# Attention and mixture-of-experts block: another order of work, and the gates sent to all partitions straight from one partition

## The chip, the cores and the metric

The kernel runs on one core of one Trainium2 chip. TensorE (PE) multiplies, VectorE (DVE), ScalarE (ACT) and GpSimd (POOL) do the rest, and SyncE (SP) issues nearly all DMAs; ACT issues a few. The metric is the time on the device in microseconds. Before the change it is 143.56 us (median of 3 runs, 143.04 to 144.24).

## The reference, cut to what matters

The input x is 4 sequences of 512 tokens of 128 values. Two residual steps follow each other:

```python
x = x + layernorm(attention(layernorm(x)))       # one head, width 128, softmax over 512 keys
x = x + layernorm(ffn(layernorm(x)))

# ffn, per token
cont   = sigmoid(h @ W_enc + b_enc) @ W_s2c + b_s2c          # 128 -> 256 -> 64
probs  = softmax(cont @ Wr + br)                             # 8 experts
gate   = the 2 largest of probs, scaled to sum 1, else 0     # [tokens, 8]
y_e    = relu(cont @ W1[e] + b1[e]) @ W2[e] + b2[e]          # 64 -> 128 -> 64, every expert
out    = sigmoid(sum_e gate[:, e] * y_e @ W_c2s + b_c2s) @ W_dec + b_dec
out    = layernorm(out) * ln_g + ln_b
```

All eight experts are computed for all tokens, and the gate scales each one's hidden layer.

## The kernel before

Each engine has its own list of instructions, written out by hand; semaphores tie them together, and no engine looks past an instruction that waits. A sequence b (0 to 3) is worked on whole: its 512 tokens are 4 tiles of 128. Attention of sequence b+2 is laced with the expert stage of sequence b, so that PE always has work; sequences 2 and 3 are left over at the end and make up the last stretch, from about 94 us on.

The change touches mainly the way of the gates. On DVE `router_top` and `router_gates` compute `gate`, 128 tokens by 8 experts for each tile. PE turns it (`turn_gates`), and ACT copies it to `gateT` (`gate_out`, L518): 8 partitions, one for each expert, with 512 floats (2 KB) in each. DVE multiplies the hidden layer of expert e, 128 partitions by 512 tokens, by the gates of that expert, so it needs that row of 512 on all 128 partitions: `gate_all[:, b % 2, e]`, two sequences deep. SP brings it there:

```python
sp.wait_ge(a_gT, b + 1)
sp.dma_start(gates_dram[b].ap(), gateT[0:E, b % 2]).then_inc(d_gate_out, 16)
sp.wait_ge(d_gate_out, 16 * (b + 1))
for e in range(E):
    sp.dma_start(gate_all[:, b % 2, e:e + 1],
                 gates_dram[b].ap()[e:e + 1].partition_broadcast(P))...
```

That is one write of 16 KB to memory (L357), a wait for it, and eight transfers of 256 KB (L362), each of which reads one row of 2 KB 128 times from memory and writes it to 128 partitions. A sequence moves 2 MB so.

`gate_hidden(b, e)` on DVE (L1158) waits for row e and for PE's hidden layer (L841, `hidden_pair`), writes `gated`, and frees both the hidden banks and, at e = 7, the buffer of rows. PE's `expert_out(b, e)` (L862) waits for `gated`. Behind `expert_out(b, 7)` PE has the scores of sequence b+3 (L729), `to_cont`, `to_spikes`, `route` for sequence b+1 and later its `turn_gates`. Behind `gate_hidden(b, 7)` DVE has the next `router_top` and `router_gates`. So the gates of sequence b+1 come after all of sequence b's expert stage for b = 0 and b = 1. Those of sequence 3 come before DVE's `gate_hidden(2, 0)`.

The end of a sequence: `decode` on PE (L887, L889), `dec_scale` (L1172) and `dec_var` (L1179) on DVE, `dec_square` on ACT (L542), the inverse deviation on POOL (L390), `z_stats` on DVE (L1187, L1052), again POOL, then for sequences 0 to 2 `z_norm` on ACT (L549) and an addition on POOL (L401), and for sequence 3 `z_centre` on ACT (L555) and `z_add` on DVE (L1201); SP stores the result (L352). A warm-up of 9 matmuls on zeros (L680) runs while the first loads arrive; then come `fold_weights` (L669 to L676) and the turning of x (L694).

Of the kernel before, what the change touches and what calls it, by code (L numbers as in the profile page):

```python
# [12 lines left out]
P = 128  # L13
EPS = 1e-5
WARM_UP = 9


def attention_moe_block(
# [26 lines left out]
    gates_dram = [nc.dram_tensor(f"gates{b}", [E, S], F32) for b in range(B)]  # L45

    with ExitStack() as ctx:
# [161 lines left out]

        def decoded(b, t):  # L210

            if b == B - 1 and t >= TH:
                return ps_a[:, t * P:(t + 1) * P]
            return (ps_t if b == B - 1 else ps_c[:, 0])[:, t * P:(t + 1) * P]

        d_x = [[sem(f"d_x{b}{i}") for i in range(1 if b else 2)] for b in range(B)]
        d_qk = sem("d_qk")
        d_wv = sem("d_wv")
# [9 lines left out]
        d_gate_out = sem("d_gate_out")  # L228
# [81 lines left out]
        v_mean = sem("v_mean")  # L310
        v_out = sem("v_out")
# [4 lines left out]
        def _(sp):  # L316
# [3 lines left out]
            for i, (t0, t1) in enumerate(HALVES):  # L320
                sp.dma_start(x_in[:, 0, t0:t1], x_dram[0, :, t0:t1]).then_inc(d_x[0][i], 16)
# [51 lines left out]
        def _(pool):  # L373
# [19 lines left out]
            def minus_means(b):  # L393
                pool.wait_ge(g_rstd[LN_Z], b + 1)
                pool.wait_ge(v_mean, b + 1)
# [3 lines left out]
            def z_add(b):  # L399
                pool.wait_ge(a_zn, T * (b + 1))  # L400
# [32 lines left out]
            for b in range(3):  # L433
                if b >= 1:
                    inverse_std(LN_DEC, b, 0)
                inverse_std(LN_Z, b, 0)
                minus_means(b)
                if b < 2:
                    z_add(b)
            inverse_std(LN_DEC, B - 1, 0)  # L440
            inverse_std(LN_DEC, B - 1, 1)
            z_add(2)
# [4 lines left out]
        def _(act):  # L447
            def w_out():
                act.wait_ge(pe_wqk, 1)
                act.wait_ge(d_qk, 64)  # L450
# [61 lines left out]
            def gate_out(b):  # L512
# [3 lines left out]
                if b >= 2:  # L516
                    act.wait_ge(d_gate_out, 16 * (b - 1))
# [27 lines left out]
            def z_norm(b):  # L545
                act.wait_ge(g_mean, b + 1)
# [5 lines left out]
            def z_centre(h):  # L552
                act.wait_ge(v_mean, B + h)
# [4 lines left out]
            for i, weight in enumerate((Wq, Wk)):  # L558
                act.dma_start(w_qkv[:, i], weight).then_inc(d_qk, 16)
            for i, bias in enumerate((bq, bk)):  # L560
                act.dma_start(b_qk[:, i:i + 1], bias.rearrange("(d a) -> d a", a=1)).then_inc(d_qk, 16)
            act.dma_start(w_qkv[:, 2], Wv).then_inc(d_wv, 16)
            act.dma_start(bv_row[:, :], bv.rearrange("(a d) -> a d", a=1)).then_inc(d_wv, 16)
# [36 lines left out]
            second_exp(0)  # L600
            values_out(2)
            for b in range(2):
                n, m = b + 1, b + 2
                more = m + 1 < B
                exps(m, 0)
                if b >= 1:
                    for c in range(HC):
# [26 lines left out]
            for c in range(HC):  # L634
                spike2(1, c)
            hT_out(3)
            second_exp(2)
            z_norm(0)
            gate_out(2)
            dec_square(1, 0)  # L640
            spike(3, 0)
            spike(3, 1)
            cont_out(3)
            second_exp(3)
            gate_out(3)
            z_norm(1)
            moe_out(2)
            for c in range(HC):
                spike2(2, c)
            dec_square(2, 0)  # L650
# [4 lines left out]
            z_norm(2)  # L655
# [6 lines left out]
        def _(pe):  # L662


            def fold_weights():
                pe.wait_ge(g_centre, 2)
                pe.wait_ge(d_qk, 64)
# [3 lines left out]
                mm.then_inc(pe_wqk, 1)  # L671
                pe.wait_ge(d_wv, 32)
                nc.tensor.matmul(ps_s[:, 1, 0:D], centre[:, :], w_qkv[:, 2], start=True, stop=False)
                nc.tensor.matmul(ps_s[:, 1, 0:D], inv_row[:, :], bv_row[:, :], start=False, stop=True).then_inc(pe_wv, 1)
                pe.wait_ge(a_wqk, 2)
# [6 lines left out]
            def turn_x(b):  # L682
# [8 lines left out]
                for bank, s0, s1 in xnT_halves(b):  # L691
# [115 lines left out]
            def turn_gates(b):  # L807
                pe.wait_ge(v_gate, 9 * (b + 1))
                for t in range(T):
                    mm = nc.tensor.transpose(gates_bank(b)[0:E, t * P:(t + 1) * P], gate[:, b % 2, t], ident[:, :])  # L810
                mm.then_inc(pe_gT, 1)

            def hidden_pair(b, p):
# [11 lines left out]
                elif b == 2:  # L825
                    if p == 0:
                        pe.wait_ge(v_gated, E + 6)
                    elif p == 1:
                        pe.wait_ge(a_gT, b + 1)
                        pe.wait_ge(v_z1, b)  # L830
# [15 lines left out]
            def expert_biases(b):  # L846
# [4 lines left out]
                if b + 2 < B:  # L851
                    pe.wait_ge(a_pT, T * (b + 3))
                else:
# [13 lines left out]
            def to_spikes(b):  # L867
# [3 lines left out]
                if b == B - 1:  # L871
                    pe.wait_ge(v_z1, b)
# [9 lines left out]
            def decode(b, t):  # L882
# [4 lines left out]
                nc.tensor.matmul(decoded(b, t), ones_bf[:, :], b_dec_stack[:, :], start=True, stop=False)  # L887
                for c in range(HC):
                    mm = nc.tensor.matmul(decoded(b, t), spikes2[:, b % 2, c, t * P:(t + 1) * P], w_dec[:, c],  # L889
                                          start=False, stop=(c == HC - 1))  # L890
                if any(t == t1 - 1 for _, t1 in parts(LN_DEC, b)):
# [4 lines left out]
            fold_weights()  # L896
            turn_x(0)
# [7 lines left out]
            turn_x(1)  # L905
            scores(0, 2)
            turn_probs(0, 1)
            attend(0, 0)
# [47 lines left out]
            for b in range(2):  # L956
# [11 lines left out]
                if b >= 1:  # L968
                    decode(b - 1, 2)
                    decode(b - 1, 3)  # L970
                attend(m, 1)
                turn_probs(m, 2)
                if more:
                    turn_x(m + 1)
                attend(m, 2)
# [396 lines left out]
```

## Time and profile before

| what | value |
|---|---|
| median of 3 runs | 143.56 us |
| the profiled execution's own time | 143.67 us |
| its span | 141.6 us |
| PE busy | 122.2 us (86%) |
| DVE busy | 89.1 us (63%) |
| ACT busy | 64.0 us (45%) |
| POOL busy | 32.8 us (23%) |
| moved by DMA | 12.29 MB, of it 8 MB rows of gates |

Busy times are those of the profiled execution; its own time is 2.07 us more than its span. The "chain" is the work that ended last, followed back from the end: it says which engine each stretch waited for.

### The profile page before, as it was taken

Reading aid. Unit: us, or ns where it says so; the run is one execution under the profiler, and the core shown is the slowest. Engines: PE = TensorE matmul, PEld = TensorE weight load, DVE = VectorE, ACT = ScalarE, POOL = GpSimd, SP = SyncE. Lnnn points to the kernel's source line nnn. Section 1 sums busy time; section 2 is a strip of 40 time slices with the busy share of each in tenths; the row PEclk is TensorE's granted clock in tenths of the full one; section 3 lists DMA queues with packets and bytes.
Section 4 is the critical chain, followed back from the end, with each engine's and each line's share of the span. In section 5 each row is a group of like instructions: output and inputs, shape, how many; then the busy total and the mean of one; then the engine's idle time right before and its main releaser. Section 6 shows DMA issues by size and latency. Waiting matters only on the chain.

```text
span 141.6 us, 2514 instructions
## 1 busy us (share of the span) xinstructions
PE 122.2 (86%) x828; PEld 80.0 (57%) x828; DVE 89.1 (63%) x377; ACT 64.0 (45%) x185; POOL 32.8 (23%) x64
## 2 busy tenths in 40 slices
PE   6989999999978999999998898999895999888000
PEld 2447787787546777544687664478362667536000
DVE  1867429788896648933444589915299930955393
ACT  0557666656626762033874600467713213314711
POOL 4453021134210232100000341032420300023352
PEclk9999999999999999999999999999999999999955
DMA  3568200000000089000002960000299497000012
GB/s 113 150 173 221 94 0 2 0 0 2 5 0 0 8 281 306 10 0 0 0 0 74 303 225 0 0 5 2 79 264 317 104 294 287 5 0 0 2 74 74
DMA packets 10428, 12.29 MB, mean 87 GB/s; under 512 B 2818, under 2 KB 5520, under 8 KB 10416
## 3 DMA queue, kind: packets, MB, share of 16 engines
q1 hardware_dynamic: 9694, 11.95, 27.2%
q10 hardware_dynamic: 722, 0.20, 0.6%
q8 instruction: 6, 0.10, 0.3%
q14 instruction: 6, 0.05, 0.1%
HBM read 11.03 MB, written 1.11 MB: 86 GB/s over the span
## 4 chain that ended last, share of the span: by engine, by line
PE 73%; DVE 11%; ACT 6%; issue 4%; POOL 3%; POOLq 1%; DVEq 0%
PE ps_o L754 11%; PE ps_s L729 10%; PE ps_t L862 10%; PE ps_t L741 5%; PE ps_s L841 5%; PE ps_c L889 4%; POOL rstd L390 3%; DVE gated L1158 3%; PE ps_t L680 3%; PE ps_o L780 3%; PE ps_a L712 2%; PE ps_c L877 2%; PE ps_c L841 2%; DVE z L1187 2%; PE ps_a L702 2%
## 5 line engine op out<-in xcount | busy, mean ns | idle before, releaser
L390 POOL TENSOR_TENSOR rstd<-var_eps,minus_half 128x2 f32<-128x2 f32 (+1 forms) x32 | 24.9, 785 | 96.2 <-DVE var_eps L1057 42.3
L1081 DVE TENSOR_REDUCE neg_max<-ps_s 128x1 f32<-128x512 f32 x16 | 10.9, 689 | 13.5 <-PE ps_s L729 13.4
L754 PE MATMUL ps_o<-v,probsT 128*128 128x128 f32 x128 | 17.4, 279 | 1.4 <-ACT probsT L483 1.4
L862 PE MATMUL ps_t<-gated,w 128*64 128x256 f32 x128 | 17.8, 393 | 0.9 <-DVE gated L1158 0.8
L754 PEld LDWEIGHTS ps_o<-v,probsT 128*128 128x128 f32 x128 | 15.7, 191 | 4.2 <-ACT probsT L483 3.4
L729 PE MATMUL ps_s<-xnT,yT 128*128 128x512 f32 x32 | 16.3, 605 | 0.3
L478 ACT ACTIVATE probs<-ps_s,neg_max 128x512 f32<-128x512 f32 x16 | 11.0, 686 | 10.5 <-DVE neg_max L1081 10.4
L862 PEld LDWEIGHTS ps_t<-gated,w 128*64 128x64 f32 x128 | 7.7, 136 | 9.8 <-DVE gated L1158 5.1
L1158 DVE SCALAR_TENSOR_TENSOR gated<-ps_s,b_minus,gate_all 128x512 f32<-128x512 f32 x16 | 11.2, 743 | 0.5 <-PE ps_s L841 0.5
L483 ACT ACTIVATE probsT<-ps_t 128x512 f32<-128x512 f32 x16 | 9.5, 593 | 3.8 <-PE ps_t L741 3.6
L741 PE MATMUL ps_t<-ident,probs 128*128 128x128 f32 x64 | 9.8, 276 | 1.4 <-ACT probs L478 1.4
L741 PEld LDWEIGHTS ps_t<-ident,probs 128*128 128x128 f32 x64 | 7.4, 141 | 5.1 <-ACT probs L478 2.9
L841 PE MATMUL ps_s<-cont,w 64*128 64x256 f32 x64 | 9.1, 402 | 0.0
L494 ACT ACTIVATE hT<-ps_a 128x512 f32<-128x512 f32 x4 | 2.4, 597 | 12.3 <-PE ps_a L766 12.3
L1158 DVE SCALAR_TENSOR_TENSOR gated<-ps_c,b_minus,gate_all 128x512 f32<-128x512 f32 x10 | 7.0, 745 | 0.3 <-PE ps_c L841 0.3
L889 PE MATMUL ps_c<-w_dec,spikes 128*128 128x128 f32 x48 | 7.1, 288 | 0.0
L841 PEld LDWEIGHTS ps_s<-cont,w 64*128 64x128 f32 x64 | 5.5, 186 | 2.7 <-issue 2.1
L729 PEld LDWEIGHTS ps_s<-xnT,yT 128*128 128x128 f32 x32 | 5.1, 190 | 3.2 <-issue 2.6
L889 PEld LDWEIGHTS ps_c<-w_dec,spikes 128*128 128x128 f32 x48 | 6.3, 192 | 0.5 <-issue 0.3
L1187 DVE SCALAR_TENSOR_TENSOR z<-z,rstd,b_all 128x128 f32<-128x128 f32 x16 | 4.6, 346 | 2.7 <-POOL rstd L390 2.6
L1100 DVE SCALAR_TENSOR_TENSOR x_mid<-ps_o,rstd,x_in 128x128 f32<-128x128 f32 x16 | 4.8, 345 | 1.9 <-POOL rstd L390 1.9
L1055 DVE BATCH_NORM_AGGREGATE mean_var<-stats 128x2 f32<-128x6 f32 x48 | 6.0, 165 | 0.0
(175 smaller groups left out, 212.7 us busy)
## 6 DMA issues: line engine op xcount, KB each, us to landing
gate_all<-gates SPq DMA_DIRECT2D x32, 256.0 KB, 5.3
x_in<-in_L_attn_x SPq DMA_DIRECT2D x3, 256.0 KB, 3.5
w<-in_L_ffn_W SPq DMA_DIRECT2D x3, 256.0 KB, 3.8
out<-x_out SPq DMA_DIRECT2D x3, 256.0 KB, 2.0
x_in<-in_L_attn_x SPq DMA_DIRECT2D x2, 128.0 KB, 2.6
out<-x_out SPq DMA_DIRECT2D x2, 128.0 KB, 1.7
w_enc<-in_L_ffn_W_enc SPq DMA_DIRECT2D x1, 128.0 KB, 2.9
w_dec_raw<-in_L_ffn_W_dec SPq DMA_DIRECT2D x1, 128.0 KB
```

What stands on the lines that cost most here:

```text
L390: nc.gpsimd.tensor_tensor(rstd[part], var_eps[part], minus_half[:, t0:t1], ALU.pow).then_inc(g_rstd[n], 1)
L478: nc.scalar.activation(probs[:, b % 2, t], ps_s[:, t % 2], ACT.Exp, bias=neg_max[:, b % 2, t:t + 1], accum_out=prob_sum[:, b % 2, t:t + 1] ...
L483: nc.scalar.activation(probsT[:, b % 2, t], ps_t[:, :].rearrange("p (k q) -> p k q", k=T), ACT.Identity).then_inc(a_pT, 1)
L729: nc.tensor.matmul(ps_s[:, t % 2], yT[:, b % 2, t * P:(t + 1) * P], xnT[:, b % 2], start=True, stop=True).then_inc(pe_s, 1)
L741: mm = nc.tensor.transpose(ps_t[:, k * P:(k + 1) * P], probs[:, b % 2, t, k * P:(k + 1) * P], ident[:, :])
L754: mm = nc.tensor.matmul(attn_out(t), probsT[:, b % 2, t, k], v[:, b % 2, k], start=(k == 0), stop=(k == T - 1))
L841: mm = nc.tensor.matmul(hidden_banks(b, e)[:, h], w1[half, e], cont[half, b % 2], start=True, stop=True)
L862: mm = nc.tensor.matmul(ps_t[h * M:(h + 1) * M, 0:SH], w2[:, e], gated[:, e, h * SH:(h + 1) * SH], start=False, stop=(e == E - 1))
L889: mm = nc.tensor.matmul(decoded(b, t), spikes2[:, b % 2, c, t * P:(t + 1) * P], w_dec[:, c], start=False, stop=(c == HC - 1))
L1081: nc.vector.tensor_reduce(neg_max[:, b % 2, t:t + 1], ps_s[:, t % 2], AX_X, ALU.max, negate=True).then_inc(v_max, 1)
L1158: nc.vector.scalar_tensor_tensor(token_halves(gated[:, e]), hidden_banks(b, e), b1_minus[:, e:e + 1], token_halves(gate_all[:, b % 2, e]), ...
L1187: nc.vector.scalar_tensor_tensor(z[:, b % 2, t], z1[:, b % 2, t], inv(LN_DEC, b, t), b_all[:, :], ALU.mult, ALU.add).then_inc(v_z, 1)
```

## The change

- The row of an expert goes to all partitions straight out of the one partition of `gateT` in which it lies. The tensor in memory, its write and the wait for it are gone. The eight transfers stay eight, of 256 KB each, issued by SP.
- `gate_out(b)` on ACT, for b = 2 and 3, now waits until the eight transfers of sequence b-2 have landed, since they read `gateT` itself.
- The decode of sequence 1 is split in halves with a PSUM bank for each; the bias of a decode is one matmul for all its tiles instead of one per tile.
- Sequences 0 and 2 are centred and added on DVE (new `z_centre`, `z_add(b, i)`) instead of on ACT and POOL. Their stores wait for `v_out`.
- The last stretch stands in another order on PE, DVE, ACT and POOL: among others `router_gates(3)` stands before the variance and the statistics of sequence 1.
- At the start the weights of q, k and v come by other queues in another order, the folding of the weights is split in three (`fold_qk`, `fold_a`, `fold_v`), and the warm-up has 7 matmuls.

```diff
-WARM_UP = 9
+WARM_UP = 7
-    gates_dram = [nc.dram_tensor(f"gates{b}", [E, S], F32) for b in range(B)]
+            if n == LN_DEC and b == 1:
+                return HALVES
...
             def store(b, i):
-                if b < B - 1:
-                    sp.wait_ge(g_out, b + 1)
+                if b == 1:
+                    sp.wait_ge(g_out, 1)
                 else:
-                    sp.wait_ge(v_out, t1)
+                    sp.wait_ge(v_out, T * (b // 2) + t1 + (T if b == B - 1 else 0))
...
                 sp.wait_ge(a_gT, b + 1)
-                sp.dma_start(gates_dram[b].ap(), gateT[0:E, b % 2]).then_inc(d_gate_out, 16)
-                sp.wait_ge(d_gate_out, 16 * (b + 1))
                 if b >= 2:
                     sp.wait_ge(v_gated, E * (b - 1))
                 for e in range(E):
                     sp.dma_start(gate_all[:, b % 2, e:e + 1],
-                                 gates_dram[b].ap()[e:e + 1].partition_broadcast(P)).then_inc(d_gate_in[b % 2][e], 16)
+                                 gateT[e:e + 1, b % 2].unsqueeze(1).to_broadcast([1, P, S])).then_inc(d_gate_in[b % 2][e], 16)
...
                 if b >= 2:
-                    act.wait_ge(d_gate_out, 16 * (b - 1))
+                    for e in range(E):
+                        act.wait_ge(d_gate_in[b % 2][e], 16 * (b // 2))
...
             hidden_pair(2, 0)
-            for t in range(T):
-                decode(1, t)
-            turn_gates(2)
             encode(3, 0)
             encode(3, 1)
+            turn_gates(2)
+            decode(1, 0)
+            decode(1, 1)
             to_cont(3)
+            decode(1, 2)
+            decode(1, 3)
+            route(3)
+            hidden_pair(2, 2)
             hidden_pair(2, 1)
-            route(3)
             expert_biases(2)
-            hidden_pair(2, 2)
             turn_gates(3)
...
+            def z_centre(b):
+                for t in range(T):
+                    nc.vector.tensor_scalar(zn[:, b % 2, t], z[:, b % 2, t], mean_var[:, LN_Z, b % 2, t, 0:1], None,
+                                            ALU.subtract).then_inc(v_zn, 1)
...
             z_stats(0, 0)
-            z_means(0, 0)
             router_top(2)
+            router_index(2)
             router_gates(2)
+            z_centre(0)
+            z_add(0, 0)
             dec_scale(1, 0)
+            dec_scale(1, 1)
+            router_top(3)
...
```

SP, from the gates of sequence 1 to those of sequence 2. Before:

```order
L357 DMA gates<-gateT 8x512 [waits a_gT]
L362 DMA gate_all<-gates 128x512 [waits d_gate_out]
L362 DMA gate_all<-gates 128x512 x7
L352 DMA out<-x_out 128x512 [waits g_out]
L357 DMA gates<-gateT 8x512 [waits a_gT]
L362 DMA gate_all<-gates 128x512 [waits v_gated,d_gate_out]
```

The same place after the change:

```order
L369 DMA gate_all<-gateT 128x1x512 [waits a_gT]
L369 DMA gate_all<-gateT 128x1x512 x7
L361 DMA out<-x_out 128x512 [waits v_out]
L369 DMA gate_all<-gateT 128x1x512 [waits v_gated,a_gT]
```

The write of the gates is gone, the source is `gateT`, and the store of sequence 0, which the next gates stand behind, now waits for DVE (`v_out`) and no longer for POOL (`g_out`).

DVE at the end, from the last `gate_hidden` of sequence 3 (the names `zn`, `x_out` are the centred and the finished values). Before:

```order
L1158 SCALAR_TENSOR_TENSOR gated<-ps_s,b_minus,gate_all 128x512 x2
L1179 TENSOR_SCALAR var_eps<-dec_square_sum 128x4
L1187 SCALAR_TENSOR_TENSOR z<-z,rstd,b_all 128x128 x4
L1052 BN_STATS stats<-z 128x6 x4
L1055 BN_AGGR mean_var<-stats 128x2 x4
L1057 TENSOR_SCALAR var_eps<-mean_var 128x4
L1194 TENSOR_SCALAR minus_mean<-mean_var 128x4
L1179 TENSOR_SCALAR var_eps<-dec_square_sum 128x2
```

After the change:

```order
L1210 TENSOR_SCALAR var_eps<-dec_square_sum 128x4
L1189 SCALAR_TENSOR_TENSOR gated<-ps_s,b_minus,gate_all 128x512 x2
L1219 SCALAR_TENSOR_TENSOR z<-z,rstd,b_all 128x128 x4
L1080 BN_STATS stats<-z 128x6 x4
L1083 BN_AGGR mean_var<-stats 128x2 x4
L1085 TENSOR_SCALAR var_eps<-mean_var 128x4
L1231 TENSOR_SCALAR zn<-z,mean_var 128x128 x4
L1241 SCALAR_TENSOR_TENSOR x_out<-zn,rstd,x_mid 128x128 x4
L1210 TENSOR_SCALAR var_eps<-dec_square_sum 128x2
```

The variance of sequence 2 moves ahead of the last two gated tiles, and eight instructions that finish sequence 2 on DVE come in before the variance of sequence 3.

## Rows read from the trace of the kernel before

**Rows 1.** The page: busy time, granted PE clock in 40 slices, GB/s in 40 slices.
```profile
PE 122.2 (86%) x828; PEld 80.0 (57%) x828; DVE 89.1 (63%) x377; ACT 64.0 (45%) x185; POOL 32.8 (23%) x64
...
PEclk9999999999999999999999999999999999999955
...
GB/s 113 150 173 221 94 0 2 0 0 2 5 0 0 8 281 306 10 0 0 0 0 74 303 225 0 0 5 2 79 264 317 104 294 287 5 0 0 2 74 74
```

**Rows 2.** Waits, all engines: who waited <- for whom: us, times, longest.
```profile
PEld ps_t L862 <- DVE gated L1158: 5.1, 11, 0.8
...
DVE gated L1158 <- PE ps_t L862: 1.9, 1, 1.9
```

**Rows 3.** Timeline of SP's queue: start, length, line, transfer, count.
```profile
47.08 0.30 SPq L357 DMA_DIRECT2D gates<-gateT  x1
48.55 3.66 SPq L362 DMA_DIRECT2D gate_all<-gates  x8
74.25 0.29 SPq L357 DMA_DIRECT2D gates<-gateT  x1
...
100.18 0.29 SPq L357 DMA_DIRECT2D gates<-gateT  x1
```

**Rows 4.** The tile of the gates: us from issue to landing of the 32 transfers.
```profile
DMA to landing us min/median/max: 3.1/5.3/6.9
```

**Rows 5.** DMA, 47.4 to 48.4 us, the write of gateT: packets, MB, share of 16 engines.
```profile
GB/s 0 0 0 0 0 0 0 0 0 0 0 0 0 0 0 0 0 82 164 82 82 0 82 82 0 0 0 82 0 0 0 0 0 0 0 0 0 0 0 0
...
q1 hardware_dynamic: 16, 0.02, 9.1%
```

**Rows 6.** DMA, 49.5 to 57.5 us, the eight transfers of sequence 0's rows.
```profile
q1 hardware_dynamic: 1152, 2.10, 80.0%
```

**Rows 7.** DMA, 138.8 to 141 us, two stores out of 128 partitions.
```profile
q1 hardware_dynamic: 288, 0.26, 35.1%
```

**Rows 8.** PE, timeline: the last expert output of sequence 0 and of 1, last decodes.
```profile
63.82 1.08 PE L862 MATMUL ps_t<-gated,w 128*64 128x256 f32 x8
...
91.76 1.08 PE L862 MATMUL ps_t<-gated,w 128*64 128x256 f32 x8
...
129.25 0.66 PE L889 MATMUL ps_t<-w_dec,spikes 128*128 128x128 f32 x4
```

**Rows 9.** DVE, timeline: four normalized tiles, gated tiles, gates, ends of sequences 2 and 3.
```profile
47.90 1.11 DVE L1064 TENSOR_SCALAR xn<-x_in,mean_var,rstd 128x128 f32<-128x128 f32 x4
...
54.13 1.41 DVE L1158 SCALAR_TENSOR_TENSOR gated<-ps_s,b_minus,gate_all 128x512 f32<-128x512 f32 x2
...
97.66 0.19 DVE L1150 TENSOR_TENSOR gate<-pick 128x32 f32<-128x32 f32 x1
...
126.93 1.14 DVE L1187 SCALAR_TENSOR_TENSOR z<-z,rstd,b_all 128x128 f32<-128x128 f32 x4 [1.13 <-POOL rstd L390]
...
129.37 0.16 DVE L1194 TENSOR_SCALAR minus_mean<-mean_var 128x4 f32<-128x4 f32 x1
133.04 0.17 DVE L1179 TENSOR_SCALAR var_eps<-dec_square_sum 128x2 f32<-128x2 f32 x1 [3.51 <-ACT dec_squares L542]
...
137.93 0.61 DVE L1201 SCALAR_TENSOR_TENSOR x_out<-zn,rstd,x_mid 128x128 f32<-128x128 f32 x2
```

**Rows 10.** The chain that ended last: start, us, what.
```profile
1.19 4.02 PE ps_t L680 x9
...
124.98 0.74 DVE gated L1158
...
130.86 1.65 ACT zn L549 x4
132.50 0.52 ACT dec_squares L542 x4
```

**Rows 11.** Windows: busy us (count) by engine, granted PE clock, DMA share, GB/s.
```profile
130.00:133.00 3.00, 1.02 (x9) 0.82 (x8) 0.00 (x0) 2.14 (x9) 0.74 (x2) 1.00 0.01 3
...
136.00:139.00 3.00, 0.00 (x0) 0.00 (x0) 2.50 (x12) 1.39 (x4) 1.49 (x2) 0.50 0.23 87
```

More of the change, by code:

```diff
@@ L432, in _ @@
                 inverse_std(LN_MID, m, 1)
[L433 to L439, printed above, removed]
+            inverse_std(LN_Z, 0, 0)
+            inverse_std(LN_DEC, 1, 0)
+            inverse_std(LN_DEC, 1, 1)
+            inverse_std(LN_Z, 1, 0)
+            minus_means(1)
+            z_add(1)
+            inverse_std(LN_DEC, 2, 0)
+            inverse_std(LN_Z, 2, 0)
             inverse_std(LN_DEC, B - 1, 0)
             inverse_std(LN_DEC, B - 1, 1)
-            z_add(2)
             inverse_std(LN_Z, B - 1, 0)
@@ L690, in turn_x @@
                     pe.wait_ge(a_v, 3)
[L691 removed]
+                for bank, s0, s1 in xnT_halves(b)[i:i + 1]:
                     for t in range(s0 // P, s1 // P):
@@ L886, in decode @@
                     pe.wait_ge(a_c2s, HC * (b + 1))
-                nc.tensor.matmul(decoded(b, t), ones_bf[:, :], b_dec_stack[:, :], start=True, stop=False)
+                last = any(t == t1 - 1 for _, t1 in parts(LN_DEC, b))
+                for t0, t1 in parts(LN_DEC, b):
+                    if t == t0:
+                        nc.tensor.matmul(decoded_bank(b, t)[:, t0 * P:t1 * P].rearrange("p (t d) -> p t d", d=D),
+                                         ones_bf[:, :], b_dec_stack[:, :].unsqueeze(1).to_broadcast([P, t1 - t0, D]),
+                                         start=True, stop=False)
                 for c in range(HC):
                     mm = nc.tensor.matmul(decoded(b, t), spikes2[:, b % 2, c, t * P:(t + 1) * P], w_dec[:, c],
-                                          start=False, stop=(c == HC - 1))
-                if any(t == t1 - 1 for _, t1 in parts(LN_DEC, b)):
+                                          start=False, stop=(last and c == HC - 1))
+                if last:
                     mm.then_inc(pe_dec, 1)
@@ L974, in _ @@
                     turn_x(m + 1)
+                if b >= 1:
+                    decode(b - 1, 2)
+                    decode(b - 1, 3)
                 attend(m, 2)
@@ L1068, in inv, with x_stats @@
                 return rstd[:, n, b % 2, t:t + 1]
-            def x_stats(b):
-                for i in range(len(parts(LN_X, b))):
-                    dve.wait_ge(d_x[b][0 if b else i], 16)
-                    statistics(LN_X, b, i, lambda t: x_in[:, b, t])
+            def x_stats(b, i=0):
+                dve.wait_ge(d_x[b][0 if b else i], 16)
+                statistics(LN_X, b, i, lambda t: x_in[:, b, t])
             def x_norm(b):
@@ L1316, in _ @@
             z_stats(0, 0)
-            z_means(0, 0)
             router_top(2)
+            router_index(2)
             router_gates(2)
+            z_centre(0)
+            z_add(0, 0)
             dec_scale(1, 0)
+            dec_scale(1, 1)
+            router_top(3)
+            router_index(3)
+            router_gates(3)
+            for e in range(4):
+                gate_hidden(2, e)
             dec_var(1, 0)
+            dec_var(1, 1)
+            for e in range(4, E):
+                gate_hidden(2, e)
             z_stats(1, 0)
             z_means(1, 0)
-            router_top(3)
-            router_gates(3)
-            for e in range(E):
-                gate_hidden(2, e)
-            gate_hidden(3, 0)
-            gate_hidden(3, 1)
+            for e in range(4):
+                gate_hidden(3, e)
             dec_scale(2, 0)
-            for e in range(2, E):
-                gate_hidden(3, e)
+            gate_hidden(3, 4)
+            gate_hidden(3, 5)
             dec_var(2, 0)
+            gate_hidden(3, 6)
+            gate_hidden(3, 7)
             z_stats(2, 0)
-            z_means(2, 0)
+            z_centre(2)
+            z_add(2, 0)
             dec_var(B - 1, 0)
```

128 lines of the change are left out of this document (76 added, 52 removed).

## The prediction

> **What bounds the kernel now.** The page first: PE is busy for 122.2 of 141.6 us, at the full granted clock until the last slices [rows 1]. So the kernel is bound by PE, with a head and a tail in which nothing is hidden. Then the waits, for the part that the change is about. DVE's `gate_hidden` needs a row of gates and a hidden layer, and what it waited for was PE, 1.9 us at L1158; PE behind it waited 5.1 us, in 11 small pieces, for DVE's own pace [rows 2]. No wait for the gates' transfers stands there. The timeline of SP's queue says why: sequence 0's way to memory and back starts at 47.08 us, the eight rows are issued by 52.2 us, half of them land within 5.3 us of their issue and the slowest within 6.9, and `gate_hidden(0, 0)` ran at 54.1 us, seven others after it [rows 3, 4, 9]. The gates come early enough, and the way through memory costs nothing on the path: from the write to the first read it is 48.55 - 47.08 = 1.5 us, four times, all hidden. What the change takes away there is worth nothing by itself; what it puts in its place has to stay as cheap.
>
> **The price of a row from one partition.** No row of the trace shows 16 DMA engines that read the same partition. Three rows stand around it.
> - The rows of gates read from memory: 1024 packets of 2 KB took 80.0% of 16 engines over 8 us, 102 us, so 0.10 us each [rows 6]. At 16 at once a row of 128 packets takes 0.8 us and a sequence's eight 6.4 us. This is the lower bound.
> - The stores out of 128 partitions: 256 packets of 1 KB took 35.1% of 16 engines over 2.2 us, 12.4 us, so 0.048 us each, 0.097 us for 2 KB [rows 7]. SBUF read over all partitions is as fast as memory. If one partition could serve only one engine at a time, a row would cost 128 x 0.097 = 12.4 us, and eight 99 us. This is the upper bound.
> - The write of `gateT` in between: 8 packets of 2 KB out of 8 neighbouring partitions took 9.1% of 16 engines over 1 us, 1.46 us, so 0.18 us each, nearly twice the others [rows 5]. Only 8 engines can have been at work, each with a partition of its own, and still they held each other up. They moved 16 KB in 11 slices of 25 ns, 0.275 us, 60 GB/s. So neighbouring partitions share a way out. If all eight rows share it, it gives 60 GB/s, and a row of 256 KB costs 4.4 us. If it is two ways with four rows on each, one way gives 30 GB/s, and a row costs 8.8 us.
>
> The change reads one partition at a time with every engine, since all 16 queues hold row 0 first, then row 1, and so on. That is the case of the third row made worse. I take 9.7 us a row, from between 8.8 and 12.4 and nearer to the first, because queued engines fill the gaps that lie between the packets of a single one. **A sequence's eight rows then take 77.6 us instead of 6.4 us.**
>
> The Trainium skill has a rule that speaks against this change. By "SBUF — State Buffer", section "Door 1: The DMA port swizzle", partitions 0 to 3 lie behind one of 16 ports and 4 to 7 behind another, and a transfer over partitions 0..3 was measured at 27.6 GB/s. A row would then take 9.5 us and the whole kernel about 402 us. The trace agrees as far as it goes (0.18 us a packet against 0.10 us), though no run so far shows a single partition.
>
> **The sum, part by part**, on the clock of the profiled execution.
> 1. Head: the two warm-up matmuls less, and q's weights on SP's queue. The warm-up holds the chain from 1.19 us for 4.02 us, 0.45 us for each of nine [rows 10]; two less save at most 0.9 us, and ACT's own start lies close behind. I take 0.8 us. Sequence 0's gates are then issued at 47.08 - 0.8 = 46.3 us [rows 3]. The changed order of turning x and the new split of the statistics stay under PE and are costed at nothing; if that cover is gone, it is some tenths.
> 2. Sequence 0. The fastest landing was 3.1 us [rows 4], of which 0.8 us is the transfer, so 2.3 us fixed. Row 7 lands at 46.3 + 2.3 + 77.6 = 126.2 us. DVE stands at `gate_hidden`, and everything behind it (PE's `expert_out`, scores, the router of sequence 1) stands too, so nothing of sequence 1's gates can start.
> 3. From there to the gates of sequence 1: one gated tile 0.75 us, and from `expert_out(0, 7)` (the second half of the row at 63.82 us, 64.3 us) to SP's issue at 74.25 us 9.95 us [rows 3, 8, 10]. Issued at 136.9 us; row 7 lands 79.9 us later, at 216.8 us.
> 4. To the gates of sequence 2: 0.75 us, and from `expert_out(1, 7)` at 92.3 us to the issue at 100.18 us 7.9 us [rows 3, 8]. New in between is SP's wait: the store of sequence 0, ahead of these gates in its queue, now waits for `z_centre(0)` and `z_add(0, 0)`, which stand behind `router_gates(2)` on DVE: 1.1 us for four tiles, as for the four normalized at 47.90 us, and two times 0.61 us [rows 9], with 0.4 us for the issue 2.8 us from the gate, against 100.18 - 97.85 = 2.3 us before. That adds 0.5 us. Issued at 216.8 + 9.15 = 225.9 us.
> 5. Sequences 2 and 3. `router_gates(3)` stands before `gate_hidden(2, 0)` in the new order, so sequence 3's rows queue up right behind sequence 2's and cost only their transfer: 225.9 + 2.3 + 155.2 = 383.4 us for the last row.
> 6. Tail. From the last `gated` at 124.98 us to the end of the span it was 16.6 us [rows 10]. In it ACT normalized sequence 2 (1.65 us from 130.86 us) before the squares of sequence 3, though the decode's first half had ended at 129.9 us [rows 8, 10]. That is gone, but DVE gets eight instructions: from the gated tile's end it needs 2.4 us for the statistics (126.93 to 129.37), 1.1 us and 1.2 us for the centring and adding, all before the variance that came at 133.04 us [rows 9]. It comes at about 131.0 us now, 2.0 us saved. Tail 14.6 us, end at 398.0 us.
> 7. PE's clock. The granted clock was 1.00 up to 133 us and 0.50, the 1.2 GHz level, from 136 us, when PE had done nothing since 131 us [rows 11]. In the new kernel PE has 0.6 us of work in each 9.7 us, so it will stand at the lower level when a sequence's last row lands. Some 17 us of PE work lie on the path (9.95 of step 3, 3 of step 4, 4 of the tail). Between nothing and twice the time, I take half: 8 us.
>
> End of the span 406 us; the profiled execution's own time was 2.07 us over its span, and 0.11 us over the median. **Forecast 408 us**, 2.8 times the time before.
>
> The added waits of `gate_out(2)` and `gate_out(3)` on ACT cost nothing: DVE has used those rows long before. The rest of the new order, the split decode and the single bias matmul included, works on a path that the rows now set; what it could bring stands in the first rival.
>
> **Rivals.**
> - *Faster: one partition is read like memory.* The engines get the row at 0.10 us a packet and the 2 MB in 6.4 us. Then the rows land earlier than before, by 1.5 us, still off the path, and only the order counts: 0.8 us at the head, 2.0 us at the tail, and in the middle about 1.5 us, since the chain of sequence 1's statistics before `router_gates(3)` is gone. 143.6 - 4.3 = 139.3 us. For it: memory does give one row to all 16 engines at full pace. Against it: [rows 5]. It decides if a row's transfer takes under about 1.2 us; from there on DVE, which needs 0.75 us a gated tile and other work between, no longer hides it.
> - *Slower, but the two groups run at once.* By the page named above rows 0 to 3 and 4 to 7 lie behind different ports. Engines that are served first would reach row 4 while the others are at row 3, and both ways would work. At best all the 60 GB/s of [rows 5] flow: 35 us a sequence, 4 x 42.4 us less, 238 us. Against it: the queues have the same order and length, so there is little to drift apart. Most of this case lies between 275 and 370 us.
> - *A weak limit*, with several engines served at once from a partition: 150 to 240 us.
> - *The transfer runs on one engine only*, since its source has one partition: 128 packets of 0.097 us, 12.4 us a row or somewhat less. The same sign and nearly the same price, and part of my case.
> - *No difference*: gains of order eaten by rows that come just late.
>
> **Numbers.** The serial case has a chance of 0.72, two groups at once 0.12, the weak limit 0.04, the faster case 0.09, no difference 0.03. With a row at 8.8 us the forecast falls by 29 us to 379; with 11 us it rises by 42 to 450, and the clock moves both by 8. The last stretch up to 12.4 us (494 us) I leave out as unlikely. 275 to 455 us holds the serial case and most of the second, 8 in 10 together; the likeliest case alone reaches from 375 to 455. Faster by over 1% 0.09, within 1% 0.03, slower 0.88; 1% is about what a measurement of this kernel can tell from no change.
>
> **What would show it.** Landings of the rows 9 to 10 us apart, the last about 80 us after the issue, 150 for sequences 2 and 3 together; DMA at some 27 GB/s (256 KB in 9.7 us) with all 16 engines busy nearly the whole time; DVE's longest waits at `gated`, for DMA; PE busy for less than a third of the span, at the half clock. If instead GB/s stand near 300 in short bursts and `gated` waits for PE as before, the faster case holds. The forecast is wrong in its step 2 if rows of a sequence land in two streams, in its step 5 if sequence 3's rows don't follow sequence 2's without a gap, and in its step 7 if the granted clock stays at 1.00.

## Result: 2.68 times the time

The changed kernel takes **385.57 us**, median of 4 runs (383.4 to 389.2), against 143.9 us before (143.04 to 144.26, 4 runs on the same chip): a ratio of 2.677, 95% interval 2.656 to 2.698. Medians are of all runs, while ratios and their intervals leave out runs that fell in a slower state of the chip, here the one of 389.2 us. The forecast was 408 us with a range of 275 to 455. The sign, the mechanism and the bound were right; the size was 22 us too high.

The page of the profile after, in the form of [rows 1]: span, busy time, granted PE clock, DMA busy tenths and GB/s in 40 slices of 9.6 us, and the chain that ended last by engine.

```profile
span 384.5 us, 2497 instructions
PE 160.5 (42%) x816; PEld 92.0 (24%) x816; DVE 94.9 (25%) x393; ACT 61.4 (16%) x177; POOL 30.4 (8%) x61
...
PEclk8999995556555796555656696555555566755556
DMA  3600088889986058989998059988888898698810
GB/s 107 170 1 1 2 27 27 29 29 33 27 27 22 0 17 27 29 27 34 27 27 27 4 45 27 27 27 32 27 27 29 41 27 28 46 28 27 43 41 28
...
SPq 54%; DMA 24%; PE 15%; DVE 4%; ACT 2%; issue 1%; ACTq 0%; DVEq 0%
```

From slice 6 on, but for the stretches between the sequences, the DMA engines are eight or nine tenths busy and move 27 GB/s in most slices, where the same copies moved some 300 GB/s in the bursts of [rows 1]. Busy engines at a tenth of the rate hold packets that don't get on: from 98 to 108 us a packet of 2 KB took 1.08 us in the trace, against 0.10 us before [rows 6]. PE does nearly the same work as before (816 matmuls, 828 before), but stands at the half clock in most slices and is busy 42% of the span.

The waits answer to [rows 2]: who waited for whom, us, times, longest.

```profile
DVE gated L1189 <- DMA gate_all<-gateT: 236.4, 30, 9.0
PEld ps_t L877 <- DVE gated L1189: 236.0, 32, 9.4
```

A wait that didn't exist before now holds 236 of 384.5 us: 30 times up to 9 us, once for nearly every one of 32 rows, and PE waits for DVE as long. The span grew by 384.5 - 141.6 = 242.9 us.

DVE's timeline, gated tiles of sequences 0 and 3 (start, us, what, and the idle time before it with its releaser), answers to [rows 9].

```profile
116.40 0.75 DVE L1189 SCALAR_TENSOR_TENSOR gated<-ps_c,b_minus,gate_all 128x512 f32<-128x512 f32 x1 [8.87 <-DMA gate_all<-gateT]
124.04 0.75 DVE L1189 SCALAR_TENSOR_TENSOR gated<-ps_c,b_minus,gate_all 128x512 f32<-128x512 f32 x1 [6.89 <-DMA gate_all<-gateT]
...
321.08 0.75 DVE L1189 SCALAR_TENSOR_TENSOR gated<-ps_o,b_minus,gate_all 128x512 f32<-128x512 f32 x1 [8.94 <-DMA gate_all<-gateT]
330.76 0.75 DVE L1189 SCALAR_TENSOR_TENSOR gated<-ps_s,b_minus,gate_all 128x512 f32<-128x512 f32 x1 [8.93 <-DMA gate_all<-gateT]
335.48 0.75 DVE L1189 SCALAR_TENSOR_TENSOR gated<-ps_s,b_minus,gate_all 128x512 f32<-128x512 f32 x1 [3.98 <-DMA gate_all<-gateT]
...
364.19 0.75 DVE L1189 SCALAR_TENSOR_TENSOR gated<-ps_s,b_minus,gate_all 128x512 f32<-128x512 f32 x1 [8.81 <-DMA gate_all<-gateT]
367.83 0.75 DVE L1189 SCALAR_TENSOR_TENSOR gated<-ps_s,b_minus,gate_all 128x512 f32<-128x512 f32 x1 [2.89 <-DMA gate_all<-gateT]
```

One row lands every 9.6 to 9.7 us, with exceptions: row 3 of sequence 3 comes 4.7 us after row 2 (335.48 - 330.76), row 7 of sequence 3 3.6 us after row 6, row 7 of sequence 0 7.6 us. These are the last rows of a group of four, 0 to 3 or 4 to 7. What the DMA engines did there is in windows of the same trace (busy us and count of PE, PEld, DVE, ACT and POOL, then granted PE clock, DMA share, GB/s).

```profile
8.00:9.00 1.00, 1.00 (x4) 0.57 (x4) 0.96 (x6) 0.47 (x1) 0.00 (x0) 0.50 0.11 18
...
98.00:108.00 10.00, 1.51 (x6) 0.56 (x8) 0.75 (x1) 0.00 (x0) 0.00 (x0) 0.50 0.89 27
...
130.00:140.00 10.00, 10.00 (x79) 8.11 (x76) 4.25 (x26) 7.04 (x20) 0.00 (x0) 0.98 0.15 6
...
296.00:302.00 6.00, 0.00 (x0) 0.00 (x0) 0.38 (x1) 0.00 (x0) 0.00 (x0) 0.50 0.80 50
...
330.00:336.00 6.00, 1.03 (x4) 0.21 (x4) 1.27 (x2) 0.00 (x0) 0.00 (x0) 0.64 0.65 54
336.00:342.00 6.00, 3.13 (x12) 1.48 (x12) 0.83 (x2) 1.14 (x8) 0.00 (x0) 0.50 0.90 27
```

Inside a group it is 27 GB/s; where the queue goes over from one group to the other it is twice that, 50 and 54, for some us. Between the sequences PE works all the time, from 124 to 130 us still at 0.50 and from 130 to 140 us at nearly the full clock.

SP's timeline, answer to [rows 3], tells how the queue paces it: the eight issues of sequence 0 last 55.34 us, where eight took 3.66 us before. The rows below put two sequences together, the first of them with SP's wait for the gates between.

```profile
47.44 55.34 SPq L369 DMA_DIRECT2D gate_all<-gateT  x8
...
47.44 145.40 SPq L369 DMA_DIRECT2D gate_all<-gateT  x16
224.32 0.36 SPq L361 DMA_DIRECT2D out<-x_out  x1
224.81 125.79 SPq L369 DMA_DIRECT2D gate_all<-gateT  x16
```

### The profile page after: what moved, and what is told of

It is laid out like the page before. It is cut to its first block, busy times and chain, and to the rows that moved or that the text cites. A ratio compares the mean times of both kernels' runs of the same rounds, so it can differ in the third digit from the quotient of the medians.

```text
span 384.5 us, 2497 instructions
## 1 busy us (share of the span) xinstructions
PE 160.5 (42%) x816; PEld 92.0 (24%) x816; DVE 94.9 (25%) x393; ACT 61.4 (16%) x177; POOL 30.4 (8%) x61
## 4 chain that ended last, share of the span: by engine, by line
SPq 54%; DMA 24%; PE 15%; DVE 4%; ACT 2%; issue 1%; ACTq 0%; DVEq 0%
SPq L369 54%; DMA gate_all<-gateT 23%; PE ps_s L738 4%; PE ps_o L763 2%; PE ps_t L750 1%; PE ps_c L892 1%; PE ps_t L877 1%; PE ps_a L800 1%; DMA w_qkv<-in_L_attn_Wk 1%; DVE gated L1189 1%; PE ps_a L711 1%; PE ps_o L711 0%; PE ps_c L789 0%; PE ps_t L909 0%; DVE x_out L1241 0%
## 5 line engine op out<-in xcount | busy, mean ns | idle before, releaser
L877 PE MATMUL ps_t<-gated,w 128*64 128x256 f32 x128 | 35.8, 659 | 211.7 <-DVE gated L1189 211.7
L877 PEld LDWEIGHTS ps_t<-gated,w 128*64 128x64 f32 x128 | 9.3, 202 | 236.0 <-DVE gated L1189 236.0
L738 PE MATMUL ps_s<-xnT,yT 128*128 128x512 f32 x32 | 18.5, 682 | 0.1
L1189 DVE SCALAR_TENSOR_TENSOR gated<-ps_o,b_minus,gate_all 128x512 f32<-128x512 f32 x6 | 4.5, 750 | 50.0 <-DMA gate_all<-gateT 43.5
L853 PE MATMUL ps_s<-cont,w 64*128 64x256 f32 x64 | 13.8, 570 | 0.0
L485 ACT ACTIVATE probs<-ps_s,neg_max 128x512 f32<-128x512 f32 x16 | 11.0, 686 | 10.7 <-DVE neg_max L1108 10.7
L506 ACT ACTIVATE spikes<-ps_o,bias_half 128x512 f32<-128x512 f32 x6 | 4.1, 687 | 38.5 <-PE ps_o L789 38.5
L789 PE MATMUL ps_o<-hT,w_enc 128*128 128x512 f32 x12 | 9.4, 925 | 0.0
L853 PEld LDWEIGHTS ps_s<-cont,w 64*128 64x128 f32 x64 | 8.0, 271 | 5.2 <-issue 4.1
L853 PE MATMUL ps_c<-cont,w 64*128 64x256 f32 x40 | 7.4, 499 | 0.0
L550 ACT ACTIVATE dec_squares<-ps_c 128x128 f32<-128x128 f32 x10 | 2.6, 279 | 27.8 <-DVE z L1202 27.8
## 6 DMA issues: line engine op xcount, KB each, us to landing
gate_all<-gateT SPq DMA_DIRECT2D x32, 256.0 KB, 30.8
```

The source lines that it names most:

```text
L485: nc.scalar.activation(probs[:, b % 2, t], ps_s[:, t % 2], ACT.Exp, bias=neg_max[:, b % 2, t:t + 1], accum_out=prob_sum[:, b % 2, t:t + 1] ...
L738: nc.tensor.matmul(ps_s[:, t % 2], yT[:, b % 2, t * P:(t + 1) * P], xnT[:, b % 2], start=True, stop=True).then_inc(pe_s, 1)
L789: nc.tensor.matmul(enc_bank(b, c), w_enc[:, c * P:(c + 1) * P], hT[:, b % 2], start=True, stop=True).then_inc(pe_enc, 1)
L853: mm = nc.tensor.matmul(hidden_banks(b, e)[:, h], w1[half, e], cont[half, b % 2], start=True, stop=True)
L877: mm = nc.tensor.matmul(ps_t[h * M:(h + 1) * M, 0:SH], w2[:, e], gated[:, e, h * SH:(h + 1) * SH], start=False, stop=(e == E - 1))
L1189: nc.vector.scalar_tensor_tensor(token_halves(gated[:, e]), hidden_banks(b, e), b1_minus[:, e:e + 1], token_halves(gate_all[:, b % 2, e]), ...
```

## Experiments

Theory: a partition is read through a way out that gives 27 GB/s however many engines ask; partitions 0 to 3 share one, 4 to 7 another. Rivals: a single partition is the limit; the queue is; the slow part is something else in the change.

**Which half of the change: two runs.** The whole change but the gates still through memory, and the kernel before with direct rows alone. The edit of the second, in SP's loop (ACT's wait before `gate_out` changes as in the whole change):

```diff
-                sp.dma_start(gates_dram[b].ap(), gateT[0:E, b % 2]).then_inc(d_gate_out, 16)
-                sp.wait_ge(d_gate_out, 16 * (b + 1))
...
-                                 gates_dram[b].ap()[e:e + 1].partition_broadcast(P)).then_inc(d_gate_in[b % 2][e], 16)
+                                 gateT[e:e + 1, b % 2].unsqueeze(1).to_broadcast([1, P, S])).then_inc(d_gate_in[b % 2][e], 16)
```

> The whole change except that the gates go through memory as before. If the direct rows make all of the slowdown, this takes about 140.5 us: 143.6 less 2 us at the tail and 1.5 us in the middle, with nothing won at the head (sequence 0's gates were issued at 47.44 us in the changed kernel, at 47.08 us before). If the new order itself costs something, it is above 144 us.

> The kernel before with nothing changed but the way of the gates: each row straight from its partition. If the rows set the time alone, the order does not matter and this takes 380 to 390 us. If the new order made it worse or better under the rows, it lies outside of that.

Order alone: 138.55 us, ratio 0.961 (0.957 to 0.964). Direct rows alone: 387.07 us, ratio 2.691 (2.678 to 2.704). So the direct rows make all of the slowdown, and the new order gains 5.4 us where rows come from memory (143.91 to 138.55, 2 us more than expected) and some 2 us where they don't (387.07 to 384.76, the changed kernel's median without the run of 389.2 us): behind a transfer there is little left for an order to bring. The costliest groups on the second kernel's page (busy us, mean ns of one; idle time before them, and its releaser) show the changed kernel's wait.

```profile
L859 PE MATMUL ps_t<-gated,w 128*64 128x256 f32 x128 | 35.4, 652 | 207.5 <-DVE gated L1155 207.5
...
L1155 DVE SCALAR_TENSOR_TENSOR gated<-ps_s,b_minus,gate_all 128x512 f32<-128x512 f32 x16 | 12.0, 751 | 108.6 <-DMA gate_all<-gateT 105.0
```

**Partition, group or queue: three runs.** Two queues, SP with rows 0 to 3 and ACT with 4 to 7; two queues with even rows on SP and odd on ACT; and one queue with the groups interleaved. Here are the first's addition to ACT's program and the third's edit.

```diff
+                for e in range(4, E):
+                    act.dma_start(gate_all[:, b % 2, e:e + 1],
+                                  gateT[e:e + 1, b % 2].unsqueeze(1).to_broadcast([1, P, S])).then_inc(d_gate_in[b % 2][e], 16)
...
-                for e in range(E):
+                for e in (0, 4, 1, 5, 2, 6, 3, 7):
```

> The changed kernel, with rows 0 to 3 issued by SP and rows 4 to 7 by ACT at the same time, so that two rows are in flight that lie in different groups of four partitions. If partitions 0 to 3 share one way out of 27 GB/s and 4 to 7 another (theory of groups), and as well if each partition has its own limit of 27 GB/s (theory of single partitions), both rows move at full pace, 38 us for a sequence: 240 to 260 us. If all such reads together get 27 GB/s, it stays at 385 us.

> As e5_two_queues_apart, but SP issues rows 0, 2, 4, 6 and ACT rows 1, 3, 5, 7, so that the two rows in flight are neighbours and lie in the same group of four. Theory of groups: they share one way out, no gain, 365 to 385 us. Theory of single partitions: 240 to 260 us, as e5.

> The changed kernel, one queue as there, with the rows issued in the order 0, 4, 1, 5, 2, 6, 3, 7. Theory of groups: an engine that is one row ahead of another is at the other way out, so the two can work at once without much drift: 240 to 330 us. If the engines keep in step whatever the order, 385 us.

282.5 us, 378.3 us and 271.5 us, one run each. The window from 60 to 80 us of the even and odd rows on two queues:

```profile
60.00:80.00 20.00, 0.00 (x0) 0.00 (x0) 0.00 (x0) 0.00 (x0) 0.00 (x0) 0.50 0.90 27
```

and that of one queue with the groups interleaved:

```profile
60.00:80.00 20.00, 4.12 (x16) 1.64 (x16) 2.14 (x8) 0.00 (x0) 0.70 (x1) 0.50 0.84 53
```

In the first, two partitions of one group are being read from two queues (201 packets of SP's queue and 112 of ACT's in the window), and the rate stays at 27 GB/s: neither the partition nor the queue is the limit. In the second a single queue reads 0 and 4, then 1 and 5, and it is 53. Two queues with a group each moved 48 GB/s at first and 56 at best:

```profile
60.00:80.00 20.00, 11.39 (x66) 8.50 (x66) 5.09 (x21) 4.77 (x15) 2.82 (x4) 0.68 0.93 48
200.00:220.00 20.00, 6.16 (x26) 2.43 (x24) 1.01 (x2) 0.59 (x1) 0.00 (x0) 0.59 0.95 56
```

Their 282.5 us miss the expected 240 to 260; ACT stood in its issues for up to 14.3 us. The limit belongs to the group of four. The 53 GB/s are those of the group borders in the changed kernel, 50 and 54.

The Trainium skill's page "SBUF — State Buffer" has a further section, "Can I just issue two DMAs to hit both halves?", by which two transfers at once, on a tile at partition 0 and on one at partition 64, serialize and gain 6%. By that the interleaved order would have stayed at 27 to 29 GB/s, an estimate; it moved 53, so for transfers that each read one partition the measurement decides.

**How far apart: four runs.** Copies of a row on several partitions, so that several ways out serve it. DVE writes `gate` 16 times over (0.69 us for 0.19 us), PE turns it into 128 partitions, ACT evicts 128 instead of 8 of them; the rows are then read from 4, 8 or 16 partitions and as many engines.

```diff
-                nc.vector.tensor_tensor(gate[:, i], pick1[:, i], pick2[:, i], ALU.add).then_inc(v_gate, 2)
+                nc.vector.tensor_tensor(gate_wide[:, i].rearrange("p t (r e) -> p t r e", e=E),
...
-                                 gateT[e:e + 1, b % 2].unsqueeze(1).to_broadcast([1, P, S])).then_inc(d_gate_in[b % 2][e], 16)
+                                 gateT[e:P:32, b % 2].unsqueeze(1).to_broadcast([4, P // 4, S])).then_inc(d_gate_in[b % 2][e], 16)
```

The others have `gateT[e:32:8]`, `gateT[e:64:8]` and `gateT[e:P:8]` there.

> As e4_src16, but the transfer of row e reads 4 partitions, e, e+32, e+64 and e+96, each for 32 destinations. Theory of single partitions: 4 x 27 GB/s, a row in 2.4 us, a sequence in 20 us, the kernel at 150 to 175 us. If partitions 32 apart share a way out too (two ways for the four), 54 GB/s, a row in 4.8 us, a sequence in 38 us, 240 to 260 us. The Trainium skill, page SBUF — State Buffer, section Door 1: The DMA port swizzle, has partitions 0 to 3 and 32 to 35 on one port and 64 to 67 and 96 to 99 on another, which is the second case.

> As the kernel with four copies 32 apart, but the four partitions that hold a row's copies stand 8 apart (e, e+8, e+16, e+24); still four DMA engines at work. Theory (ways out go by groups of partitions, 32 apart shares or nearly shares): now every copy has a way of its own, 4 engines at 0.10 us a packet give 80 GB/s, a row takes 3.3 us, the queue is through with 8 rows in 26 us; span 262.8 - 32 x (5.35 - 3.3) = 197 us, between 185 and 215. Rival (the 49 GB/s of the kernel with copies 32 apart was the limit of four engines, not of ways out): again 5.35 us a row and 260 to 265 us.

> As the kernel with four copies 8 apart, with eight copies of a row, 8 apart (e, e+8, ... e+56) and eight engines. Theory (partitions 32 apart share a way out, so that eight copies stand on four ways of 27 GB/s): at most 108 GB/s, a row 2.4 us or more, a sequence's rows 19 to 22 us, span 165 to 190 us. Rival (each copy has a way of its own, 32 apart too): eight engines at 0.10 us a packet, 160 GB/s, a row 1.6 us, eight in 13 us, span 140 to 155 us.

> The changed kernel, but gateT holds the 8 rows 16 times over, in all 128 partitions (the sum of the two picks is written 16 times side by side, 0.5 us more on DVE for each sequence; PE and ACT work on 128 partitions at the same cost), and the transfer of row e reads 16 partitions, every eighth, each for 8 destinations. If the limit lies in the partitions read (one partition or its close neighbours), the sixteen sources lift it: the rows land within some 10 us, and the time is 139 to 144 us, as e1. If reading a row over and over from SBUF is slow wherever it lies, it stays near 385 us.

264.6 (above the 240 to 260 of the second case), 175.5, 180.4 us (one run each) and 139.28 us (ratio 0.968, 0.964 to 0.972). A window of each while rows flow: four copies 32 apart,

```profile
60.00:64.00 4.00, 3.13 (x12) 1.48 (x12) 1.50 (x8) 0.00 (x0) 0.69 (x1) 0.50 0.24 49
```

four copies 8 apart,

```profile
55.00:65.00 10.00, 5.98 (x44) 3.02 (x42) 3.83 (x11) 1.16 (x2) 0.69 (x1) 1.00 0.27 100
```

eight copies 8 apart,

```profile
55.00:65.00 10.00, 7.78 (x61) 5.09 (x62) 5.62 (x18) 1.41 (x6) 2.12 (x3) 1.00 0.49 107
```

and sixteen.

```profile
50.00:54.00 4.00, 4.00 (x29) 2.76 (x28) 2.75 (x12) 1.82 (x6) 1.52 (x3) 1.00 0.97 212
```

Four engines, all busy (0.24 and 0.27 of 16), move 49 GB/s from e, e+32, e+64, e+96 and 100 from e, e+8, e+16, e+24. So distance decides, not the number of engines. Eight engines on e to e+56 bring 107, hardly more than four: the copies at e+32 to e+56 add no way out. So 0 and 32 share one and 0 and 64 don't, which also fits the 49 GB/s of the first (two ways of 27); no run read such a pair alone. With the 16 copies there are eight ways, and 212 GB/s is 8 x 26.5. The span of the four copies 8 apart (173.6 us) came out below the expected 185 to 215: I had taken 0.10 us a packet, and 4 engines at 100 GB/s need 0.08. The eight copies' rows began at 50.3 us, 3.6 us later than the four's: its PE was slow in the head, 1.19 us for the four matmuls at 4.80 us against 0.68 us, though the granted clock is 1.00 there in both traces. The cause of that is open.

The port table of the Trainium skill's page "SBUF — State Buffer", section "Door 1: The DMA port swizzle", says just this: partitions 0 to 3 and 4 to 7 have a port each, +32 stays on a port, +64 changes it, 8, 16 and 24 further on are other ports, some 27 GB/s each. The runs agree with it in every pattern tried.

**Better versions: three runs.** In the changed kernel and with order alone, PE's granted clock was 0.50, the 1.2 GHz level, in the head. The window from 8 to 9 us of order alone:

```profile
8.00:9.00 1.00, 1.00 (x4) 0.57 (x3) 0.96 (x6) 0.54 (x2) 0.00 (x0) 0.50 0.12 21
```

The first `project_y` and scores, from 7.84 us on, took 1.99 and 2.52 us. So: order alone with the nine warm-up matmuls of before; that kernel with the gates' write issued by ACT; and the sixteen copies with nine warm-ups. The edits of the first two, the second against the first:

```diff
-WARM_UP = 7
+WARM_UP = 9
...
-                sp.dma_start(gates_dram[b].ap(), gateT[0:E, b % 2]).then_inc(d_gate_out, 16)
+                act.dma_start(gates_dram[b].ap(), gateT[0:E, b % 2]).then_inc(d_gate_out[b], 16)
```

> As e1_order_only, with 9 warm-up matmuls instead of 7. The trace of the changed kernel shows the granted clock at 0.50 from 8 to 10 us (1.00 in the kernel before), and y and the first scores took 1.4 us longer there. If the short warm-up is the cause, the clock stays at 1.00 and this is 0.5 to 1.2 us faster than e1 (two more matmuls cost up to 0.9 us, of which 0.55 us lies in a wait for a load). If the gaps behind the warm-up are the cause, the dip stays, and it is equal or up to 0.5 us slower.

> As e3_order_warm9 (137.47 us), but the write of the gates to memory is issued by ACT right behind its copy, not by SP. In e3 the write for sequence 3 was issued at 105.04 us and the first read only at 109.37 us, 4.3 us later instead of 1.5, since it stood in the same queue behind the 2 MB of rows of sequence 2, and DVE waited 2.7 us for rows. If the queue is the cause, the write lands in some 1.5 us again, DVE's waits for rows fall under 1 us, and the time is 1 to 2.5 us less: 135 to 136.5 us. If the 16 DMA engines are simply busy and serve the other queue no sooner, nothing changes; ACT pays 0.3 to 0.5 us per issue either way.

> As e4_src16 (139.28 us) with 9 warm-up matmuls. What 9 matmuls brought e3 over e1, about 1 to 2.4 us, it should bring here as well: 137 to 138.3 us. That is a rival to e9 for the best version: there is no way through memory at all, but DVE pays 0.5 us more for each sequence and a row takes 1.25 us instead of 0.8. If the missing round trip were worth more than that, it would be under 136 us.

137.47 us (ratio 0.957, 0.952 to 0.962), 137.52 us (0.955, 0.952 to 0.959) and 138.99 us (0.966, 0.963 to 0.969). The clock of the first of them stays up in the same window:

```profile
8.00:9.00 1.00, 0.87 (x5) 0.43 (x4) 0.96 (x6) 0.75 (x2) 0.00 (x0) 1.00 0.14 26
```

`project_y` and the scores take 1.43 and 1.88 us, and sequence 0's gates are issued at 46.16 us instead of 47.41. The gain is about 1 us, and the intervals of 0.957 and 0.961 overlap. In the sixteen copies it is 0.3 us, less than expected. That kernel showed no dip with seven warm-ups either. Of the nine traces with seven warm-ups four have the dip (the changed kernel, order alone, even and odd rows on two queues, one queue interleaved), and of the three with nine none. Over whole runs of order alone and of the sixteen copies with seven, four of 12 had a mean granted clock of 0.966 to 0.976, and none of the 18 runs with nine was below 0.980. So seven leave the dip to the execution; that nine rule it out is likely by these counts, not shown. The issue by ACT gained nothing, against the 1 to 2.5 us expected, and its reason fell. With order alone, sequence 3's write comes while sequence 2's rows are still under way:

```profile
101.37 3.66 SPq L373 DMA_DIRECT2D gate_all<-gates  x8
106.30 0.28 SPq L368 DMA_DIRECT2D gates<-gateT  x1
110.54 4.49 SPq L373 DMA_DIRECT2D gate_all<-gates  x8
```

It takes 4.2 us until the first row is issued instead of 1.5, and DVE waits 2.1 us for rows in all. I took the queue for the cause. From ACT's queue the write was issued at 105.16 us and the rows still followed at 109.36. The DMA windows of that trace, 105.2 to 107.8 us and 107.8 to 109.2 us, show the queues at work, q1 SP's and q10 ACT's (packets, MB, share of 16 engines):

```profile
q1 hardware_dynamic: 418, 0.77, 76.4%
...
q1 hardware_dynamic: 174, 0.30, 56.2%
q10 hardware_dynamic: 16, 0.02, 3.3%
```

The write's first packet starts at 107.88 us, 2.7 us after its issue, and each of its eight packets of 2 KB then takes 0.084 us. The write of sequence 2's gates had only a store of 256 KB beside it; its packets started 1.35 us after the issue and took 0.12 to 0.29 us each. So the write waits, in either queue, for its turn behind the transfers that are under way, and not at the way out, where its packets would have been drawn out. Whether the engines or the handing over of the packets to them holds it stays open. The lowest median is that of order as changed, gates through memory and nine warm-ups: **137.5 us**, 4.3% below before (ratio 0.957), though not clear of order alone.

## Why the prediction was right, and where its size was off

- **Price of a row (9.7 us taken).** 9.6 us measured. The rows gave 8.8 to 12.4 us, and that the choice within it was right to 1% is partly luck. Its source, the 0.18 us a packet of [rows 5], had shown the shared way already: where the eight packets of such a write started apart, at 107.88 to 108.81 us, each took 0.084 us. The rival of a single engine is out, since 0.89 of 16 engines were busy.
- **Step 1 (issue at 46.3 us).** It came at 47.44 us, 1.1 us late, with the clock at 0.50 from 8 to 10 us, which I had costed at nothing. Where the clock stayed up the term was right: the kernel with two queues apart has the same head with seven warm-ups, no dip, and issued its rows at 46.16 us, and so did order alone with nine warm-ups its write. Seven and nine give the same time there, so the 0.9 us (47.08 to 46.16) come from the rest of the new head and not from the warm-ups, as I had it.
- **Steps 2 and 3's rows (79.9 us from issue to last row).** 76.6 and 76.5 us. 8 x 9.6 + 2.3 would be 79.1; the other 2.5 us is the overlap of the groups: row 3 came 9.05 us after row 2 and row 7 7.6 after row 6.
- **Steps 3 and 4, the work between (10.7 and 9.15 us).** 124.04 to 137.44 is 13.4 us, 213.94 to 224.81 10.87 us. The excess of 4.4 us goes to step 7.
- **Step 5 (157.5 us for sequences 2 and 3): the one that failed in size.** 224.81 to 367.83 is 143.0 us. Row 0 of sequence 3 did follow without a gap, but I had ruled out that the two groups run at once ("there is little to drift apart"). They do at the borders, and the more the longer the queue is: the last row of a group came 0.5 and 2.0 us early in a sequence alone, 0.6 and 1.8 in sequence 2, and 9.6 - 4.7 = 4.9 and 9.6 - 3.6 = 6.0 us early in sequence 3. The windows of 50 and 54 GB/s show the overlap and the interleaved order its full size. That some engines get ahead and reach the next group earlier can be seen in when the 16 parts of a row land. The parts of sequence 0's row 3 land from 86.84 to 87.52 us. Of row 4, the first row of the other group, one part is there at 88.09 us, while the last comes at 97.08. Within the sequence the lead doesn't close again, and a longer queue lets more parts run ahead: the first part of sequence 3's row 0 lands at 296.80 us, when row 7 of sequence 2 still lands (296.17 to 301.53 us), and its last at 311.31.
- **Step 6 (tail of 14.6 us).** 384.5 - 367.83 = 16.7 us, with the clock in it. With order alone, where the clock is out of it, the last gated tile began at 123.2 us and the tail was 137.0 - 123.2 = 13.8 us, against 16.6 before: 2.8 us gained, where 2.0 were forecast.
- **Step 7 (8 us of clock).** It is taken by difference: what steps 3, 4 and 6 took beyond their terms is 2.7 + 1.7 + 2.1 = 6.5 us. In step 3 `expert_out(0, 7)` took 1.12 us for four matmuls, against 1.08 us for eight [rows 8], and the first scores after row 7 took 3.78 us, against 1.98 before, at a granted clock of 0.50; that is most of its 2.7 us:

```profile
125.89 3.78 PE L738 MATMUL ps_s<-xnT,yT 128*128 128x512 f32 x4
```

Summed against 406: +1.1, -3.3 and -3.4 (rows), -14.5 (step 5), +6.5 - 8 (clock) = 384.4 us, the span to 0.1.

The faster rival's 139.3 us came from the order's gains, and order alone gave 138.55: the sizes were about right, their places not. The head lost 0.3 us (gates issued at 47.41 instead of 47.08 us), the last gated tile still came 1.8 us earlier, and the tail brought 2.8: 4.6 us of span. In the middle DVE came to `gate_hidden(2, 0)` 2.7 us earlier, since `router_gates(3)` no longer stands behind the waits and statistics of sequence 1. Sequence 3's gates were issued 2.7 us earlier too, but its rows only 0.1 us (110.54 against 110.66 us), and DVE's 2.1 us of waits for rows are new. The gated tile `(2, 0)` before and with order alone:

```profile
107.61 1.41 DVE L1158 SCALAR_TENSOR_TENSOR gated<-ps_s,b_minus,gate_all 128x512 f32<-128x512 f32 x2
...
104.92 1.41 DVE L1192 SCALAR_TENSOR_TENSOR gated<-ps_s,b_minus,gate_all 128x512 f32<-128x512 f32 x2
```

With order alone DVE had the decode's variance at 128.75 us instead of 133.04 [rows 9].

```profile
128.75 0.17 DVE L1213 TENSOR_SCALAR var_eps<-dec_square_sum 128x2 f32<-128x2 f32 x1
```

The rival that two groups run at once was not all or nothing, as I had it, but a share: 18 us out of the rows' 32 x 9.6 = 307.

## What to carry to other kernels

A broadcast out of SBUF is paid by the source's ways out, not by bytes: before a detour through memory is removed, ask how many groups of partitions the data stands on, for 256 KB cost 9.6 us from one of them and 0.8 us from memory. If the data must come from SBUF, put copies where the groups differ (8 apart, or 64, not 32) or order the transfers so that neighbours use different groups; sixteen copies came within 1.5 us of memory. A small write in front of a broadcast that is issued while megabytes are under way lands only when they are nearly through, whichever queue takes it: making its data ready earlier, by 2.7 us here, brought the rows forward by 0.1 us.

## What the runs showed of the hardware

- One group gives 27 GB/s to 16 engines that are 0.9 busy; two groups gave 48 to 56, four 100 to 107, eight 212.
- An issue can block: a row landed 30.8 us after the start of its issue, three rows' time, and from the fourth on SP's issue lasted as long as a row. The tile's row of the changed kernel (ns min, median, max; first and last start):

```profile
L369 SPq DMA_DIRECT2D gate_all<-gateT x32: 470/9550/9633, 47.4 to 341.0; - x32
...
DMA to landing us min/median/max: 11.8/30.8/32.2
```

- With ACT as the second queue this blocking stood in ACT's own program, so its other work waited up to 14.3 us for an issue. Before its `probs` stand 49.8 us in all in which it waited for no other engine ("issue"):

```profile
L485 ACT ACTIVATE probs<-ps_s,neg_max 128x512 f32<-128x512 f32 x16 | 11.0, 686 | 58.3 <-issue 49.8
```

  That this is why two queues (282.5 us) lost to one queue interleaved (271.5 us) is likely; no run shows it alone.
- A write of 16 KB takes 4.2 us from its issue to the first read behind it with 2 MB of other transfers under way, 1.5 us without, in the same queue or another.
